# Attention between ScalarE's exponentials: sources of the masked merge copied to SBUF, weight splits held behind GpSimd's masks, and another table of TensorE's turns

## The reference

```python
x = x + attn(layernorm(x)); x = x + ffn(layernorm(x))
# attn: 32 heads of 8 columns, 8 heads of keys and values (each serves 4 query heads)
scores = q @ k.T / sqrt(8)
amask = where((j >= i - 128) & (j < i), -1e10, 0)        # a band of 128 below the diagonal is shut out
out = softmax(scores + amask) @ v @ wo
# ffn: sigmoid router, the best 2 of 8 experts by weight, and 2 shared experts, each silu(x wg) * (x wu) @ wd
```

## Time and profile before

| | |
|---|---|
| median of 3 runs | 965.64 us (964.86 to 968.94) |
| the profiled execution | 964.84 us, its span 963.2 us |
| granted TensorE clock, mean | 0.982 |
| busy in the span | PE 93%, ACT 61%, DVE 48%, POOL 32% |
| busy in 228 to 256 us, one group | PE 26.42, ACT 26.91, DVE 11.80, POOL 11.93 us of 28 |

### The profile page before, as it was taken

The page is one execution under the profiler, slowest core; times in us unless marked ns, Lnnn a source line. Parts: engine busy times, 40 slices in busy tenths (PEclk is TensorE's granted clock), DMA queues, the critical chain, the costliest instruction groups (busy, mean ns, idle before and its releaser), DMA issues.

```text
span 963.2 us, 24188 instructions
## 1 busy us (share of the span) xinstructions
PE 897.6 (93%) x8205; PEld 567.9 (59%) x8206; DVE 462.7 (48%) x766; ACT 584.3 (61%) x729; POOL 308.4 (32%) x420
## 2 busy tenths in 40 slices
PE   8869999999999999999997999999998999999994
PEld 5423333333333333333336888888887888888883
DVE  7654443344444433444455777656753344343332
ACT  3679999999999999999992423342222222222221
POOL 6004443443444434434440000000012545444442
PEclk9979999999999999999997999999999999999998
DMA  5254444555544455532022106100027873655522
GB/s 170 85 165 153 146 160 163 200 202 198 188 155 143 162 178 199 203 95 87 16 55 72 44 22 229 43 24 22 1 71 257 264 206 75 180 153 147 148 39 22
DMA packets 42095, 123.80 MB, mean 129 GB/s; under 512 B 7624, under 2 KB 23112, under 8 KB 35904
## 3 DMA queue, kind: packets, MB, share of 16 engines
q1 hardware_dynamic: 30288, 109.50, 33.2%
q0 software_dynamic: 7008, 9.70, 6.0%
q10 hardware_dynamic: 4752, 4.01, 1.3%
HBM read 74.03 MB, written 49.15 MB: 128 GB/s over the span
## 4 chain that ended last, share of the span: by engine, by line
PE 69%; issue 8%; DVE 7%; POOL 6%; ACT 5%; SPq 3%; DMA 1%; POOLq 0%; DVEq 0%; ACTq 0%
PE ps L1584 15%; PE ps L1728 14%; PE ps L1537 11%; PE ps L1682 11%; PE ps L1747 7%; POOL arena L758 6%; PE ps L1695 5%; ACT arena L906 4%; DVE ps L1086 4%; PE ps L1738 2%; PE ps L1633 1%; SPq L525 1%; SPq L528 1%; PE ps L1709 1%; PE ps L1669 1%
## 5 line engine op out<-in xcount | busy, mean ns | idle before, releaser
L906 ACT ACTIVATE arena<-ps 128x1024 f32<-128x1024 f32 x336 | 316.7, 1044 | 9.8 <-PE ps L1537 9.8
L758 POOL TENSOR_SCALAR_AFFINE_SELECT arena<-arena 128x512 f32<-128x512 f32 x240 | 184.2, 780 | 294.7 <-ACT arena L917 194.6
L1584 PE MATMUL ps<-arena 128*32 128x256 f32 x4096 | 269.1, 386 | 5.6 <-POOL arena L758 5.0
L1537 PE MATMUL ps<-arena 64*128 64x512 bf16 (+1 forms) x1280 | 181.9, 342 | 20.2 <-ACT arena L906 8.7
L1584 PEld LDWEIGHTS ps<-arena 128*32 128x32 f32 x4096 | 110.7, 109 | 117.7 <-issue 45.4
L1086 DVE COPY_PREDICATED ps<-keep,ps 128x512 f32<-128x512 int32 (+1 forms) x128 | 80.5, 629 | 168.8 <-PE ps L1537 168.8
L1537 PEld LDWEIGHTS ps<-arena 64*128 64x128 bf16 x1280 | 53.5, 94 | 167.6 <-ACT arena L906 79.6
L1728 PE MATMUL ps<-wr_all,x2T 128*128 x648 | 144.8, 364 | 6.0 <-issue 3.9
L1728 PEld LDWEIGHTS ps<-wr_all,x2T 128*128 128x128 f32 x648 | 105.6, 189 | 28.4 <-issue 14.0
L917 ACT ACTIVATE arena<-ps 128x1024 f32<-128x1024 f32 x112 | 114.7, 1039 | 8.9 <-DVE ps L1086 4.7
L1682 PE MATMUL ps<-x2T,wr_all 128*128 128x512 f32 x480 | 118.7, 399 | 1.2 <-issue 1.2
(11 more groups left out here) (182 smaller groups left out, 746.0 us busy)
## 6 DMA issues: line engine op xcount, KB each, us to landing
w_scr<-wr_all SPq DMA_DIRECT2D x24, 1280.0 KB, 7.0
wr_all<-w_scr SPq DMA_DIRECT2D x24, 1280.0 KB, 5.8
raw<-w_experts SPq DMA_DIRECT2D x24, 640.0 KB, 7.2
arena<-q_scr SPq DMA_DIRECT2D x64, 64.0 KB
o_scr<-arena SPq DMA_DIRECT2D x128, 32.0 KB, 1.6
arena<-o_scr SPq DMA_DIRECT2D x16, 256.0 KB, 4.2
raw<-w_shared SPq DMA_DIRECT2D x6, 640.0 KB, 4.2
arena<-q_scr SPq DMA_DIRECT2D x32, 96.0 KB
```

The lines of the kernel that those rows point to most:

```text
L758: nc.gpsimd.affine_select(out=dst, in_=src, compare_op=ALU.is_ge if own else ALU.is_gt, fill=0.0, base=0, pattern=[[0, REP], [-1 if own el ...
L906: nc.scalar.activation(prob[:, SLOT[unit(a, kt)], :, :].rearrange("p h q -> p (h q)"), score.rearrange("p b x -> p (b x)"), ACT.Exp, scale ...
L1537: return nc.tensor.matmul(ps[:, bank, :].rearrange("p (h q) -> p h q", h=2)[:, :, place * P:(place + tiles) * P], kst[r0:r0 + HALF, s, kt ...
L1584: last = nc.tensor.matmul(ps[32 * h:32 * h + 32, 6 + qc, a % 2 * QW:(a % 2 + 1) * QW], vst[:, s, kt, :], prob[:, SLOT[k], h, :], start=(no ...
```

## The change

- `merge_pair`: DVE first copies the source of the first half from PSUM to `x_first` in SBUF (128 x 512, for a = 0 half of it) and signals `x_copied`; the first predicated copy reads `x_first`, the second the bank as before. PE's second source waits for `x_copied` instead of the first predicated copy.
- `group` of DVE: it waits for the group's last mask before `split_part(g, 0)`.
- `TURNS` has 17 turns for 14; the order of the scores is unchanged.
- The bias moves from a row of `qst` to a row of `kst`, half as long (1024 columns for 2048); the row of `qst` against it holds ones, which ACT fills once at the start in two copies of 4096 elements (`ones_out`). SP no longer waits for the rows, nor stores a fill of them (`shift_fill`); PE waits for them itself.
- Set-up: the norms of chunk c + 2 are made inside `last_parts(c)` on DVE, ACT moves the transposed x of chunk c + 1 out earlier, and takes over the copy of the values (`values_out`). Pool's band and keep masks wait for the norms of all chunks.

Of the diff, the lines that do this (declarations and the shift of two start rows are left out):

```diff
@@ -27,10 +27,11 @@
+FIRST_PART = 1 + SHIFT_ROWS
...
-assert PAIR_ROWS + SHIFT_ROWS <= HALF
+assert PAIR_ROWS + FIRST_PART <= HALF
@@ -109,19 +110,22 @@
-TURNS = (((3, 4), ((3, 4, 1), (3, 5, 1), (0, 3))),
-         ((5, 7, (0, 0)), ((0, 2),)),
-         ((6, (0, 1), 8), ((0, 4), (0, 5), (0, 6))),
+TURNS = (((3,), ((3, 3, 1), (3, 4, 1), (3, 5, 1), (0, 3))),
+         ((4, 5, 7, (0, 0)), ((0, 2),)),
+         ((6, (0, 1), 8), ((0, 6), (0, 5), (0, 4))),
...
-         ((11, (1, 1)), ((1, 0), (1, 4), (1, 5))),
-         ((13, (2, 0), 14, 15), ((1, 6), (0, 0), (0, 1))),
-         ((16, 18), ((1, 2),)),
-         ((17, (2, 1), 19), ((1, 7), (1, 1), (1, 3), (2, 0))),
-         ((20, 21, (3, 0), 23), ((2, 1),)),
-         ((22, (3, 1)), ((2, 2), (2, 4))),
-         ((24, 25), ((2, 7), (2, 5), (2, 6))),
-         ((26, 27), ((2, 3), (3, 0), (3, 1))),
-         ((28, NEXP, NEXP + 1), ((3, 2), (3, 3), (3, 7), (3, 6))),
+         (((1, 1), 11), ((0, 0), (1, 0), (1, 5))),
+         ((13, 14, (2, 0), 15), ((1, 6), (0, 1), (1, 4))),
+         ((16, (2, 1), 18), ((1, 7),)),
+         ((17,), ((1, 2), (1, 3), (1, 1))),
+         ((19, 20), ((2, 0),)),
+         (((3, 0), 21, 23), ((2, 1),)),
+         ((22, (3, 1)), ((2, 6), (2, 3))),
+         ((24, 25), ((2, 5),)),
+         ((26,), ((2, 2), (2, 4), (2, 7), (3, 0))),
+         ((27, 28), ((3, 6),)),
+         ((NEXP,), ((3, 1),)),
+         ((NEXP + 1,), ((3, 7), (3, 2))),
@@ -542,7 +547,7 @@
-                    r0, n0 = half * HALF, half * (REP // 2 * KT)
+                    r0, n0 = half * HALF + 1, half * (REP // 2 * KT)
@@ -560,19 +565,11 @@
-                sp.wait_ge(shift_low, 2)
-                sp.wait_ge(shift_high, 2)
...
-                    sp.wait_ge(shift_low, s + 1)
-                    sp.wait_ge(shift_high, s + 1)
...
-                sp.wait_ge(u_bias, 1)
-                sp.dma_start(shift_scr[:, 0].rearrange("n r q -> n (r q)").rearrange("n (y x) -> n y x", x=512),
-                             shift_fill).then_inc(shift_stored, 16)
-                sp.wait_ge(shift_stored, 48 + FIRST)
@@ -737,6 +734,8 @@
+            pool.wait_ge(vaug_ready, 1)
+            pool.wait_ge(a_xn, NC)
@@ -855,33 +854,52 @@
                     nc.scalar.copy(parts[0:r, qc, m, 0, :], ps[0:r, 2 + m, :]).then_inc(a_p0, 1)
+                    if m == 2:
+                        between()
                     act.wait_ge(a_p0, c * 3 + m + 1)
...
+            def values_out(c):
+                b, qc = divmod(c, QC)
+                act.wait_ge(vaug_ready, 1)
+                act.wait_ge(a_v, c + 1)
+                nc.scalar.copy(vaug[:, b * KV:(b + 1) * KV, qc * TPC:(qc + 1) * TPC, 0:HD],
+                               ps[:, 5, 0:TPC * KV * HD].rearrange("p (t g d) -> p g t d", t=TPC, g=KV)).then_inc(a_vsb, 1)
...
                 act.dma_start(dst, w.rearrange("(k p) n -> p k n", p=P)).then_inc(w_in, 16)
+            def ones_out(half):
+                row = slice(half * HALF, half * HALF + 1)
+                nc.scalar.copy(qst[row, :, :, :].rearrange("p s h q -> p (s h q)"),
+                               ones_row[row, 0:1].to_broadcast([1, REP * L])).then_inc(qst_ones, 1)
+            act.wait_ge(qst_zero, 1)
+            act.wait_ge(ones_ready, 1)
+            ones_out(0)
             root(1)
...
             root(2)
+            ones_out(1)
             for c in range(NC):
-                first_parts(c)
-                if c + 1 < NC:
-                    xT1_out(c + 1)
+                first_parts(c, (lambda: xT1_out(c + 1)) if c + 1 < NC else (lambda: None))
                 if c + 2 < NC:
                     root(c + 3)
+                values_out(c)
             store_parts(act, NC - 1)
...
             act.wait_ge(const, N_CONST)
+            act.wait_ge(ones_ready, 1)
             nc.scalar.activation(exp_of_one[0:1, :], ones_row[0:1, 0:1], ACT.Exp)
...
             for s in range(2):
-                nc.scalar.copy(qst[HALF:HALF + 1, s, :, :].rearrange("p h q -> p (h q)"),
-                               ps[HALF:HALF + 1, 7, 128:129].to_broadcast([1, REP // 2 * L])).then_inc(shift_high, 1)
+                nc.scalar.copy(kst[HALF:HALF + 1, s, :], ps[HALF:HALF + 1, 7, 128:129].to_broadcast([1, L])) \
+                    .then_inc(shift_high, 1)
@@ -983,38 +1001,59 @@
             nc.vector.memset(squares[KV * HD:P, :, 2, :], 0.0).then_inc(first_const, 1)
-            nc.vector.memset(qst[:, :, :, :].bitcast(F32), 0.0).then_inc(const, 1)
+            nc.vector.memset(qst[:, :, :, :].bitcast(F32), 0.0).then_inc(qst_zero, 1)
             nc.vector.memset(kst[:, :, :], 1.0).then_inc(const, 1)
-            def norm1(c):
-                dve.wait_ge(x_in[c], 16 if c else 32)
-                layernorm(dve, lambda t: xres[:, c * TPC + t, :], lambda t: xn1[:, c % 2, t, :], c * A_LN, 0, a_xn, c + 1)
-            def last_parts(c):
-                b, qc = divmod(c, QC)
+            def rows_of(c, t):
+                return xres[:, c * TPC + t, :]
+            def row_stats(c, tiles):
+                if 0 in tiles:
+                    dve.wait_ge(x_in[c], 16 if c else 32)
+                for t in tiles:
+                    nc.vector.bn_stats(stats[:, t, :], rows_of(c, t)).then_inc(dve_step, 1)
+            def row_variances(c):
+                for t in range(TPC):
+                    wait_apart(dve, dve_step, c * A_LN + t + 1)
+                    nc.vector.bn_aggr(meanvar[:, t, :], stats[:, t, :]).then_inc(dve_step, 1)
+                dve.wait_ge(dve_step, c * A_LN + 2 * TPC)
+                nc.vector.tensor_scalar(rstd[:, :], meanvar[:, :, 1], EPS, None, ALU.add).then_inc(ln_var, 1)
+            def rows_out(c):
+                dve.wait_ge(ln_sd, c + 1)
+                nc.vector.reciprocal(rstd[:, :], rstd[:, :]).then_inc(dve_step, 1)
+                dve.wait_ge(dve_step, c * A_LN + 2 * TPC + 1)
+                for t in range(TPC):
+                    nc.vector.tensor_scalar(xn1[:, c % 2, t, :], rows_of(c, t), meanvar[:, t, 0:1], rstd[:, t:t + 1],
+                                            ALU.subtract, ALU.mult).then_inc(a_xn if t == TPC - 1 else dve_step, 1)
+            def last_parts(c, ahead):
+                qc = c % QC
                 for m in range(3):
...
                                             ALU.subtract).then_inc(a_rem, 1)
+                    if ahead and m < 2:
+                        row_stats(c + 2, range(m * TPC // 2, (m + 1) * TPC // 2))
+                    if ahead and m == 2:
+                        row_variances(c + 2)
                     dve.wait_ge(a_p1, c * 3 + (m + 1 + 3))
...
                                             ALU.subtract).then_inc(a_p2, 1)
-                dve.wait_ge(vaug_ready, 1)
-                dve.wait_ge(a_v, c + 1)
-                nc.vector.tensor_copy(vaug[:, b * KV:(b + 1) * KV, qc * TPC:(qc + 1) * TPC, 0:HD],
-                                      ps[:, 5, 0:TPC * KV * HD].rearrange("p (t g d) -> p g t d", t=TPC, g=KV)) \
-                    .then_inc(a_vsb, 1)
+                if ahead:
+                    rows_out(c + 2)
                 dve.wait_ge(a_norm, c + 1)
...
-            norm1(0)
-            norm1(1)
+            for c in range(2):
+                row_stats(c, range(TPC))
+                row_variances(c)
+                rows_out(c)
             for c in range(NC):
-                last_parts(c)
-                if c + 2 < NC:
-                    norm1(c + 2)
+                last_parts(c, c + 2 < NC)
             dve.wait_ge(a_p2, NC * 3)
@@ -1037,10 +1076,7 @@
-                nc.vector.tensor_copy(qst[0:1, s, :, :].rearrange("p h q -> p (h q)"),
-                                      ps[0:1, 7, 128:129].to_broadcast([1, REP // 2 * L])).then_inc(shift_low, 1)
-            dve.wait_ge(shift_high, 2)
-            nc.vector.tensor_copy(shift_fill, ps[:, 7, 128:129].to_broadcast([P, 512])).then_inc(u_bias, 1)
+                nc.vector.tensor_copy(kst[0:1, s, :], ps[0:1, 7, 128:129].to_broadcast([1, L])).then_inc(shift_low, 1)
@@ -1073,15 +1109,26 @@
+            def sides_of(a):
+                return slice(0 if a else 1, 2)
+            def halves_of(bank, a):
+                return ps[:, bank, :].rearrange("p (h s q) -> p h s q", h=2, s=2)[:, :, sides_of(a), :]
...
-                sides = slice(0 if a else 1, 2)
+                sides = sides_of(a)
                 for bank in range(2):
                     if bank == 0:
+                        wait_apart(dve, x_ready, g * NMERGE + (2 * a + 1))
+                        nc.vector.tensor_copy(x_first[:, sides_of(a), :, :].rearrange("p s h q -> p h s q"),
+                                              halves_of(X_BANK[a], a)).then_inc(x_copied, 1)
+                        wait_apart(dve, x_copied, g * QP + (a + 1))
                         wait_apart(dve, s_ready, g * NEXP + (ISSUE_NO[MERGED_AT[a]] + 1))
-                    wait_apart(dve, x_ready, g * NMERGE + (2 * a + bank + 1))
```

(20 more changed lines are left out.)

21 lines of the change are left out of this document (11 added, 10 removed).

## The result

The changed kernel takes 960.08 us in the median of 9 runs (956.94 to 968.93), the kernel before beside it 964.86 (9 runs, 964.01 to 968.94): ratio 0.9948, with 95% interval 0.9925 to 0.9972. It is faster by 0.5%, about 5 us, where 15 were forecast. The profiled execution is the quickest, 956.94 us with a span of 955.3.

What follows compares the result with a forecast made beforehand. ACT's exponentials were taken to bound each attention group, 27.63 us falling to 26.7; sixteen groups gave 14.9 us and the set-up 0.5, so 15.4 off 964.84, forecast 950 us. The range was 941 to 961, the forecast's own 945 to 956.

Steps and rivals of the forecast that it cites:

- signs of being wrong: PE idle ahead of a second source, first predicated copies over 1 us, SP's release after 60, ACT idle ahead of exponential 11.
- The bound and the floor: Attention: ACT's exponentials need 25.81 of a group's 27.63 us; only its four stalls, 1.79 us, can be had.
- The hold: End of group: DVE splits after the last mask, masks run undisturbed, the 0.75 us stall at exponential 2 goes; priced at nothing.
- The new turns: PE's order in attention: new stalls of 0.15, 0.26 and 0.12 us, making a group 26.34, about 26.4 with changes of form.
- The walk by buffers and windows: Timeline of PE's scores in a group: each must start after its buffer is freed and 0.50 us ahead of its exponential.
- Where DVE and Pool meet: Merges: first predicated copy, now reading two SBUF tensors, may wait for Pool's masks; 0.3 us a group taken, bounds nothing to 1.3.
- one full meeting: Merge 3: first predicated copy beside Pool's third mask of unit 2 waits up to 0.77 us, 0.49 over its margin.
- The rival of the port: Attention merges: copies wait through more than one mask, 984 us; decides from 1.3 us a group beyond margins; chance 0.04 slower, 0.05 even.
- The copy of the sources: Merges: the second source issues at once, first predicated copy to exponential takes 1.52 us for 2.10; 1.04 us a group gone.
- three merge stalls: ACT's waits in a group at merges: 0.31, 0.43 and 0.30 us ahead of 238.99, 244.87 and with the pair from 248.50.
- The set-up: Before the first scores: chunk 1 ends some 0.5 us earlier; 0.5 gained, bounds 0.6 lost and 2.2 gained.
- The sum: Whole kernel: 14.9 us from sixteen groups and 0.5 from set-up, 15.4 off 964.84; median 0.8 above that execution, 950.2.

Runs made afterwards that it cites:

- Hold and copy with the old table: Kernel before plus the wait of the splits and the source copy in `merge_pair`, with the old table of turns: 953.24 us, ratio 0.9874.
- the whole with three repairs: Changed kernel with copies of ones behind chunks 1 and 2, two masks waiting for predicated copies, values (2, 2) and (2, 5) exchanged: 949.83 us, 0.9834.

## Why the prediction was wrong

It had the sign and the mechanisms of attention, and 960 lies inside its range, but the size was off by a factor of three (5 us for 15). Two terms of the sum failed, the meetings of DVE and Pool by their size and the set-up by its sign; its own signs of being wrong, first predicated copies over 1 us and a release after 60, both came. Point by point:

- **The bound and the floor** held. ACT's exponentials are 25.81 us of each group in all traces, and the stages behind attention did not move.
- **The hold** held: the masks take 0.63 us each, the splits start behind the last of them and run at their shortest (0.83 and 1.49), nothing waits for them. Alone it gives 27.15. And its cover is real: without it the change is 32 us slower than before.
- **The new turns** held: 0.28, 0.14 and 0.13 measured for 0.26, 0.12 and 0.15. The walk by buffers and windows is good to 0.02 us. Exponential 11, with 0.03 to spare, was in time.
- **Where DVE and Pool meet** is the step that failed, by its size. It had "one full meeting" and took 0.3. Two cost: 0.36 ahead of 12 and 0.20 ahead of 23, 0.56. Merge 3's was foreseen (0.49 at most, 0.20 came). Merge 1's was priced at a wait of 0.03, as the copy would come when Pool's second mask ends. That mask ended at 233.44 and the source's copy at 233.37, but the predicated copy starts 0.34 us behind the source's copy, at 233.71, and by then the third mask had begun (233.61): 1.08 us for 0.70. In the gap ahead of that mask it would have taken 0.70, by the rows of "Hold and copy with the old table": little more than 0.1 us decided. Keeping these two masks away removed exactly both stalls. The difference is 0.26 us a group, 16 x 0.26 = 4.2 us. The rival of the port had the mechanism, but its point, beyond 1.3 us over the margins, was not reached. The Trainium skill, SBUF — State Buffer, section Who interferes with whom, has a VectorE instruction with two SBUF inputs contend with a GpSimd instruction that reads SBUF, and the order of issue decide who blocks: the traces agree, with 0.70 us undisturbed and 1.08 behind a mask, and with a mask of 1.12 for 0.63 behind a copy.
- **The copy of the sources** was sized at 1.04 us, three merge stalls in full. Without it, and with the new table, these stalls are 0.28, 0.42 and 0.28, 0.98 in all, so there was that to take. With it they are 0.36, none and 0.20, as the port gives 0.56 back, and 0.14 comes ahead of 17: 0.98 less 0.70 is 0.28, and the periods say 0.33.
- **The set-up** is the other step that failed, by its sign: "I take 0.5" gained, "bounds 0.6 lost" and "2.2 gained"; 2.9 were lost. The root was put 0.7 late and came 3.0 late. The first table load stood at 4.13 in the trace before, with nothing to wait for, and stands behind the waits of the copy now, at 4.93, so that the copy ends at 9.82 and not at "about 8.8": 1.0. Then comes a second load ahead of the root, 1.28, as the copy has taken the first: 2.3 in all. The Trainium skill, ScalarE activation tables: per-element evaluation and per-set limits, section What a function is on this engine, has a load of 1283 ns between functions of different sets; the 1.28 us of both loads agree. Why a copy ahead of the root brings a load of its own is not shown: in the trace before the copies behind the root run without one. The second copy, put at 1.3 on the path, was hidden, but only as the clock held PE back by 2.5, a term that the sum did not have. Chunks are quicker afterwards, and 2.7 of the 5.5 are left at SP. With both copies behind chunks 1 and 2 the set-up gains 0.4 against the trace before, and 0.6 by the means of three and five traces, near the 0.5 of the forecast: the place of the copies is the loss. The clock's part of it is partly luck: the same fall came with the set-up of before in two of five traces, and the one that the forecast was read from had none. A third way, Pool's memset, showed nothing on this, as it held DVE instead.
- **The sum.** Forecast 15.4 less. Attention gave 10.9 for 14.9, 4.0 short, of which the port is 4.2; the set-up 3.4 short. That leaves 8.0, for 7.9 measured in the profiled execution. The median lies 3.1 above that execution, where 0.8 were assumed, another 2.3; with it 9.7 of the 9.9 us between 950.2 and 960.08 are accounted for. Executions of this same kernel differ by the stretches of lower clock in the set-up, at the end of attention and behind it. The stages behind attention take 459 to 461 us for 457 in 6 of the 12 traces of edited kernels other than that without the hold, and not in the one of before; why is open, no run here was made for it. (Of the 2.9 us at the first score only 0.6 are left at exponential 12 of the first group; the rest stands in attention's 10.9.)

## What to carry to other kernels

When an operation gets a second SBUF operand, look up in the timeline where it will start against GpSimd's instructions. If one runs then, count what is left of it; if the start falls in a gap, even one of 0.16 us, the operation goes first and GpSimd's next instruction is the one that waits. Where 0.1 us decides, as here, move the mask or the operation, with what waits for them. Put nothing on ACT ahead of the first function on the path without looking where the table loads will stand. Compare stages over several traces, as two traces with the same set-up were up to 3 us apart here. And try the parts alone: here one line held more than the whole, and the whole with three repairs held three times as much.

## What the runs showed of the hardware that was not expected

- A predicated copy with mask and data in SBUF waits for a GpSimd mask that runs when it starts (what is left of the mask and 0.55 us, up to 1.17, for 0.70 alone), and a mask waits for such a copy that started before it (1.12 us for 0.63), even in a gap of 0.16 us between masks. With its data in PSUM the copy does not wait (0.70 at most in 64, of which 17 of full size started during a mask).
- A GpSimd memset that writes one partition only, 1 x 2048, blocked DVE's norming in SBUF for as long as it ran: 4.54 us for 1.38.
- With 4.24 us without work on PE in the set-up the granted clock was 0.66 in the mean from 10 to 20 us, and eight transposes took 1.97 us for 1.09; with the unchanged set-up it stayed at 2.4 GHz where PE stood for 0.48 to 1.06 us and fell where it stood for 1.30 and 2.10; in executions of one and the same kernel, stretches of lower clock came or stayed away behind attention, worth 2 to 4 us.
